# A two-layer state-space block with a channel mix: the logarithm of the step sizes moved behind the fourth chunk's exponential, and what follows it on VectorE and GpSimd moved to the second half of the block

## What is computed

```python
zxbcdt = u @ in_w.T
z, xBC, dt = jnp.split(zxbcdt, [D_INNER, D_INNER + CONV_DIM], axis=-1)   # 1024, 1152, 16
dt = jax.nn.softplus(dt + dt_bias)                   # the step sizes
xBC = silu(conv(xBC) + conv_b)                       # depthwise, 4 taps
xh, Bm, Cm = jnp.split(xBC, [D_INNER, D_INNER + D_STATE], axis=-1)
dA = jnp.exp(dt * -jnp.exp(A_log))
# over the tokens t, for 16 heads of 64 x 64:
state = dA_t * state + (dt_t * x_t) B_t
y_t = state C_t
# behind it
y = (y + D * xh) * silu(z)
y = y * rsqrt(mean(y * y) + EPS) * rms_w
h = y @ out_w.T + res
```

## Time and profile before

| | |
|---|---|
| median of three runs | 4333.67 us |
| the profiled execution's own time | 4342.61 us |
| its span, first to last instruction | 4340.8 us |
| TensorE matmul busy | 4017.9 us, 93% |
| VectorE busy | 3475.0 us, 80% |
| ScalarE busy | 2908.6 us, 67% |
| GpSimd busy | 2027.6 us, 47% |
| granted TensorE clock, mean | 0.961 of full speed |

### The profile page before, as it was taken

One profiled execution on the slowest core, in us unless ns is written; L12 is line 12 of the kernel. 1 busy time (PEld: TensorE's weight loads), 2 busy tenths in 40 slices (PEclk: granted clock), 3 DMA queues, 4 the chain that ended last, 5 costly groups with the idle time before them and its releaser, 6 DMA issues. The chain is left out here.

```text
span 4340.8 us, 100166 instructions
## 1 busy us (share of the span) xinstructions
PE 4017.9 (93%) x38872; PEld 3611.2 (83%) x38872; DVE 3475.0 (80%) x5217; ACT 2908.6 (67%) x4904; POOL 2027.6 (47%) x1572
## 2 busy tenths in 40 slices
PE   4499999999999999958999999999999995799989
PEld 1399989898989899958999999999999994677777
DVE  8588888888888888867888888888888885576664
ACT  4577767676767677746777777777777773666655
POOL 7344444444444444423444444444444444556664
PEclk6699999999999999979999999999999997899999
DMA  8300000000000000020000000000100002122220
GB/s 326 136 31 31 31 31 31 31 31 31 30 31 30 31 31 31 26 97 26 31 31 31 31 33 30 31 31 34 39 31 30 31 26 96 71 93 93 91 74 35
DMA packets 108579, 220.18 MB, mean 51 GB/s; under 512 B 10760, under 2 KB 11272, under 8 KB 107272
## 3 DMA queue, kind: packets, MB, share of 16 engines
q1 hardware_dynamic: 108176, 214.25, 13.8%
HBM read 146.97 MB, written 67.24 MB: 49 GB/s over the span
## 5 line engine op out<-in xcount | busy, mean ns | idle before, releaser
L503 PE MATMUL l_ring<-l_u_hi,l_wi_lo 128*128 128x256 f32 x4608 | 1318.9, 286 | 43.1 <-DVE l_u_lo L933 29.0
L503 PE MATMUL l_ring<-l_u_lo,l_wi_hi 128*128 128x256 f32 x4608 | 1297.5, 282 | 0.0
L503 PE MATMUL l_ring<-l_u_hi,l_wi_hi 128*128 128x256 f32 x4608 | 1296.8, 281 | 0.0
L985 DVE SCALAR_TENSOR_TENSOR l_xc<-l_raw,l_prm,l_xc 128x256 f32<-128x256 f32 x1536 | 952.8, 664 | 115.1 <-ACT l_xc L761 96.9
L503 PEld LDWEIGHTS l_ring<-l_u_hi,l_wi_lo 128*128 128x128 f32 x4608 | 874.5, 190 | 67.9 <-issue 29.8
L503 PEld LDWEIGHTS l_ring<-l_u_lo,l_wi_hi 128*128 128x128 f32 x4608 | 874.8, 190 | 12.9 <-issue 1.3
L503 PEld LDWEIGHTS l_ring<-l_u_hi,l_wi_hi 128*128 128x128 f32 x4608 | 874.8, 190 | 0.0
L1169 POOL TENSOR_TENSOR l_g<-l_g 128x512 f32<-128x512 f32 (+2 forms) x384 | 355.4, 926 | 1096.8 <-ACT l_g L822 1076.7
L1140 POOL TENSOR_TENSOR l_rhs<-l_cum,l_small 32x1024 fp32r<-32x1024 f32 x256 | 497.1, 1950 | 214.5 <-PE l_wide L565 145.2
L1160 POOL TENSOR_TENSOR l_g<-l_g,l_zs 128x1024 f32<-128x1024 f32 x128 | 305.8, 2389 | 452.2 <-DVE l_g L1032 450.6
L503 PE MATMUL l_ring<-l_wo_hi,l_g_lo 128*128 128x512 f32 x1024 | 414.1, 404 | 18.9 <-DVE l_g_lo L1037 11.5
(11 more groups left out here) (175 smaller groups left out, 8104.1 us busy)
## 6 DMA issues: line engine op xcount, KB each, us to landing
l_hn<-h_scratch SPq DMA_DIRECT2D x64, 512.0 KB, 3.8
l_res<-h_scratch SPq DMA_DIRECT2D x128, 256.0 KB, 3.6
h_scratch<-l_res SPq DMA_DIRECT2D x128, 256.0 KB, 2.1
m_rows<-in_x SPq DMA_DIRECT2D x16, 1024.0 KB, 9.4
h_scratch<-m_rows SPq DMA_DIRECT2D x16, 1024.0 KB, 7.3
f_x<-in_x SPq DMA_DIRECT2D x16, 1024.0 KB, 7.0
f_h<-h_scratch SPq DMA_DIRECT2D x16, 1024.0 KB, 8.9
out<-f_x SPq DMA_DIRECT2D x64, 256.0 KB, 2.0
```

The source lines that it names most:

```text
L503: last = nc.tensor.matmul(out, a, c, start=(k == 0), stop=(k == n - 1))
L985: ins = nc.vector.scalar_tensor_tensor(out=acc, in0=raw[:, (s + c) % 2, k, tap:tap + TB], scalar=prm_sb[:, w:w + 1], in1=acc, op0=ALU.mult ...
```

## The change

In the block (not in the start of a layer, where the order stays as it was) three lists change. On ScalarE the logarithm leaves `step_exp` and becomes `step_ln`, called behind the fourth chunk's `decays`. On VectorE `steps` and `sum_parts` go behind the fourth chunk's `matrices`. On GpSimd `inv_rms(b, s, 0)` goes ahead of `moving(*nxt, 0)`, and `moving(*nxt, 1)` behind `gate(b, s, 1)`. No instruction is added apart from table loads, no operand or shape changes, and TensorE's list stays.

```diff
@@ ScalarE, step_exp
                 nc.scalar.activation(dty, dty, ACT.Exp, scale=-1.0).then_inc(s_exp, 1)
+
+            def step_ln(b, s):
+                i = NB * b + s
                 act.wait_ge(s_exp, i + 1)
                 nc.scalar.activation(dty, dty, ACT.Ln, bias=1.0).then_inc(s_ln, 1)
@@ ScalarE, body
                 decays(b, s, 1, 1)
                 if n1:
+                    step_ln(*nxt)
                     z_read(*nxt, 2)
@@ ScalarE, start of a layer
             step_exp(b0, 0)
+            step_ln(b0, 0)
             conv_in(b0, 0, 0)
@@ VectorE, body
                 matrices(b, s, 0, 0)
-                if n1:
-                    steps(*nxt)
                 y_read(b, s, 0, 0)
...
                 if n2:
                     row_stats(*nxt2)
                 if n1:
-                    sum_parts(*nxt)
                     taps(*nxt, 1)
                 y_read(b, s, 1, 0)
                 matrices(b, s, 1, 1)
                 if n1:
+                    steps(*nxt)
+                    sum_parts(*nxt)
                     stationary_sums(*nxt)
@@ GpSimd, body
                 if n2:
                     inv_std(*nxt2)
+                inv_rms(b, s, 0)
                 if n1:
                     moving(*nxt, 0)
+                gate(b, s, 1)
+                if n1:
                     moving(*nxt, 1)
-                inv_rms(b, s, 0)
-                gate(b, s, 1)
                 squares(b, s, 1)
```

## The result

The changed kernel takes **4561.9 us**, median of 4 runs (4559.8 to 4562.9); the kernel before, run beside it, takes 4333.6. The ratio is 1.0523, with a 95% interval of 1.0507 to 1.0539: **slower by 5.2%**. The forecast was 4576, with a range of 4460 to 4660.

The account below looks back on a forecast made before the run. TensorE, with next to no idle time, bounds the kernel. 62 blocks x (2.6 wait + 1.3 clock) = 242 us takes the profiled 4342.6 to 4585, the median to 4576 us; range 4460 to 4660.

Parts of the forecast that it names:

- nil slack of `low_g(b, s, 1)`: VectorE, ahead of TensorE's second-pair out product: any delay of it delays the block, hastening it gives back 0.3 us at most.
- The saved table loads: ScalarE at `decays`: 62 loads of 1.28 us go, 79 us, but TensorE's own work hides the saving.
- The moved `steps` and `sum_parts` are absorbed: VectorE's second half: 1.66 us came, 1.60 and 0.61 of waiting went, so `y_read(b, s, 1, 1)` starts as before.
- What GpSimd costs: 2.6 us: VectorE's twelve taps, held by GpSimd's two `moving` and gate, end 2.6 us later per block, making the out product late.
- The other bound, 3.2: Upper bound per block at the twelve taps: above 3.2 us if the time GpSimd holds them adds in full.
- The wait of 2.9 us: TensorE at the out product: existing 0.3 plus 2.6 added gives 2.9 us idle per block.
- The clock, 1.3 us a block: TensorE's clock behind that wait falls in three of four blocks at 1.7 us, so 1.3; bounds 0 and 2.1.
- The waits at the back edge: TensorE's 11 unexplained waits at L541, 19.6 us in all, may come and go; worth about 20 us and the clock.
- the same wait at full clock: Rival: TensorE's out product waits 2.6 us more per block without a clock fall, 161 us, 4495; chance 0.26.
- the gain of `low_g`: Rival: VectorE's chain gets shorter and TensorE's 0.3 us closes, 19 us, 4315; chance 0.08 together with ScalarE's 79 us.
- ScalarE's 79 us: Rival: the saved table loads come through in full, 4255; chance 0.08 together with the gain of `low_g`.
- no difference: Rival: GpSimd takes 1.66 us from the taps as now, 4334; would need `moving(1)` behind the taps; chance 0.06.

Follow-up runs that it names:

- experiment 3: The changed kernel with one more wait: GpSimd's `moving(1)` waits for `low_g` of the second pair; 4425.1 us, ratio 1.0199.
- experiment 5: The kernel before with `inv_rms(b, s, 0)` alone moved ahead of both `moving`, the gate staying behind them; 4552.5 us, ratio 1.0499.
- experiment 6: The kernel before with the gate alone moved ahead of `moving(1)`, `inv_rms` between `moving(0)` and the gate; 4409.8 us, ratio 1.0171.
- experiment 10: Like experiment 9, with `taps(*nxt, 2)` on VectorE ahead of `y_read(b, s, 1, 1)` as well; 4326.8 us, ratio 0.9979 to the kernel before.
- experiment 2: The kernel before with the change to GpSimd's list alone; logarithm, `steps` and `sum_parts` stay where they were; 4564.1 us, ratio 1.0521.
- experiment 1: The changed kernel with GpSimd's list put back to that of the kernel before, ScalarE and VectorE as changed; 4492.1 us, ratio 1.035.
- experiment 7: The kernel before with `sum_parts` behind `y_read(b, s, 0, 1)` and both `moving` behind `gate(b, s, 0)`, in the first half; 4459.4 us, ratio 1.0281.
- experiment 9: Like experiment 7, but `sum_parts` one step further ahead, in front of `y_read(b, s, 0, 1)`; 4334.0 us, ratio 0.9998 to the kernel before.
- experiment 4: The changed kernel with `moving(0)` and `moving(1)` cut to one head of 16, leaving work out; 4311.4 us, ratio 0.9942 to the kernel before.
- Experiment 8: Like experiment 7, with `taps(*nxt, 2)` on VectorE ahead of `y_read(b, s, 1, 1)` as well; 4447.3 us, ratio 1.0258 to the kernel before.

## Why the prediction was right

- **The bound: nil slack of `low_g(b, s, 1)`.** Right for a delay. After the change, and in experiments 3, 5 and 6, the out product starts 0.14 to 0.15 us behind its end, block by block. For a gain it wasn't: experiment 10 closed the gap and TensorE waited elsewhere.
- **The saved table loads are worth nothing.** Right: experiment 2 keeps all 126 loads at `decays` and takes as long as the change without 62 of them (ratio 1.0521 against 1.0523).
- **The moved `steps` and `sum_parts` are absorbed.** Right in the changed kernel: VectorE waits for TensorE at `y_read(b, s, 1, 1)`, by 0.48 us, and the first instruction takes 0.42 us. Experiment 1 limits it: with GpSimd's old list the same move costs 3.5%.
- **What GpSimd costs: 2.6 us.** The mechanism right, the size a little small: 9.78 - 6.95 = 2.83 us. The part that failed is "both sides alternate, one tap between two GpSimd instructions". Between the gate and `moving(1)` a tap got in (it starts at 1267.85). Between `moving(0)` and the gate none did, and the first tap was held through both, 3.36 us. The taps begin 1.26 us behind `y_read`, as before, so only the held time differs. The other bound, 3.2, would have needed no tap in between at all.
- **The wait of 2.9 us.** Measured 2.95 on the mean. But the block grew by 2.52 only, since 0.3 us closed at L565: 60 x 2.52 = 151 us in the 60 blocks counted above, where the sum has 2.6 a block and nothing for L565. Two slips cancel here by luck: the held time was 0.2 too small, and the closing wait was left out.
- **The clock, 1.3 us a block.** Measured 56.50 - 54.90 = 1.6, or 96 us in 60 blocks, where the sum had 81 in 62. The prediction took it from three stretches, "a fall in three of four blocks at 1.7"; in the trace it fell in 57 of 60, and the out product is slower there by 1.3 to 2.8 us. It was the least certain term. Experiments 6 and 3 show that it could have been nothing: behind waits of 1.75 us and of 1.3 the clock stayed at 1.00.
- **The waits at the back edge** "may come and go": they went, 19.6 us down to 0.3. The 60 blocks of the kernel before take 3174.4 us, 32 us more than 60 x 52.38, most of it in five blocks of layer 0 that take 57.3 to 59.1 us, with the wait and the clock behind it. Named in the range, not in the sum.
- The sum for the 60 blocks: 151 + 96 - 32 = 215 us, and 3389.8 - 3174.4 = 215. The two profiled executions differ by 218 in all and the medians by 228, since that of the kernel before lay 9 us above its median. The forecast had 242: some 32 too much for the back edges and 10 for the wait, 15 too little for the clock. So the nearness of 4576 to 4561.9 is in part errors that cancel.
- Of the rivals, the same wait at full clock (4495) is excluded by the windows above, the gain of `low_g` (4315) by 62 waits, ScalarE's 79 us (4255) by experiment 2, and no difference (4334) "would need `moving(1)` behind the taps", which is experiment 3: even then it is 2% slower.

## What to carry to other kernels

Before an instruction of GpSimd that reads SBUF is moved, look at what VectorE does beside its new place. Where VectorE's taps, with two operands from SBUF, stood beside GpSimd's products, the two ran one after the other, and what counted was only whether the chain behind had slack. The SBUF — State Buffer page of the Trainium skill (Who interferes with whom) states that an instruction of VectorE with two inputs in SBUF contends with one of GpSimd that reads SBUF, and for the taps every experiment here agrees; a held time is a little shorter than the instruction: 1.65 us for a `moving` of 2.08, 2.02 for a gate of 2.38. And an instruction that waits for another engine (`inv_rms` here, 0.54 us of work) is a barrier in its queue: moving it ahead moves all that stood before it to a later time, here at a price of 5%.

## What the runs showed that was not expected

- **GpSimd can get its turn twice in a row.** The first tap stood ready when `moving(0)` ended at 1225.81 in experiment 3, and the gate got the next turn. In the changed kernel too, but there a tap got in between the gate and `moving(1)`. What decides it isn't shown.
- **It isn't only instructions with two large operands of SBUF.** In experiment 7 it was a TENSOR_SCALAR of 128x256 with a small second operand, 2.37 us instead of 0.35; in experiment 1 L930, 2.49 instead of 1.00. `y_read`, `finish` and the products of `x_read`, which read PSUM, ran beside GpSimd in their usual time. Nor does every product of GpSimd hold VectorE up: the first instruction of `steps` took 0.42 us in the changed kernel at 1258.49, while GpSimd's product of 128x2 is shown as under way (L1136, 1258.36 to 1259.07; GpSimd's spans are rough).
- **Waits at the loop's back edge come and go with the lists of the other engines.** TensorE's own list is the same in all kernels. Its wait at L541 for nothing that the profile shows (us in total, times, longest), in experiments 1, 7, 9 and 10:

```profile
PE l_ps_m L541 <- issue: 20.3, 12, 3.9
```

```profile
PE l_ps_m L541 <- issue: 16.9, 11, 3.7
```

```profile
PE l_ps_m L541 <- issue: 12.5, 11, 3.7
```

```profile
PE l_ps_m L541 <- issue: 6.7, 12, 0.7
```

In the kernel before and in experiment 1, with GpSimd's old list, a wait of 3.2 to 3.9 us stands in every fourth block through most of the first layer; in the kernel before such a block takes 57.3 to 59.1 us. With the new list the waits are 0.3 us in all in the change and in experiment 3, at most 0.4 in experiment 4, and four of 0.9 to 2.7 in experiment 2. GpSimd's list isn't all of it: experiments 7 and 8 have the same one, as have 9 and 10, and in each of these pairs only VectorE's `taps(.., 2)` moved, with the long waits there in the first and gone in the second (at most 0.7). Experiment 8 has the same 6.7 us as 10. A pause of TensorE in each block isn't what keeps them away either: experiment 4 has none beyond that of before and no such wait over 0.4, and experiments 1 and 7 have pauses and the waits. In the kernel before, the wait from 842.3 to 845.9 has two whole microseconds in which no DMA transfer is shown. In experiment 4 the five blocks take 24 us less than before, which is most of what it gains, 28 us; in the tenth they take 24 us less too, and other blocks more. The cause stays open: nothing here separates the place of the code from the time at which the other engines end their trip.
